# Sinkhorn reciprocals written to PSUM, sums made by accumulating DMAs, and a new order around the stream mixes of a two-layer attention and FFN kernel

## What is computed

```
x = x + fake_quant(LN(x)) @ fake_quant(ctx)                  # layer 1
x = x + mixed(LN(x)) + branch(LN(x))                         # layer 2
x = x + softmax((LN(x) Wq' + bq)(ctx Wk' + bk)' / 32) @ ctx  # layer 3
x = x + down(silu(gate(LN(x))) * up(LN(x)))                  # layer 4, hidden size 2752, low-rank terms added

# layer 2, per token, x_streams = LN(x) as 4 streams of 256:
H_res = sinkhorn_log(logits, 50 iterations, tau 0.1)         # 4x4, rows and columns normalised in turn
H_res = (1 - g) * I + g * H_res
x_mixed = einsum('btij,btjc->btic', H_res, x_streams)
y = einsum('btnc,btn->btc', x_streams, H_pre) @ W_branch
result  = x_mixed + einsum('btc,btn->btnc', y, H_post)
```

## Time and profile before

| | |
|---|---|
| time before | 1239.46 us, median of 3 runs (1236.49 to 1240.28) |
| the profiled execution's own time | 1237.51 us |
| its span, first to last instruction | 1235.7 us |
| TensorE busy (matmuls) | 1169.7 us, 95% |
| VectorE busy | 797.1 us, 65% |
| ScalarE busy | 479.5 us, 39% |
| GpSimd busy | 128.9 us, 10% |
| mean granted TensorE clock | 0.986 of full |

### The profile page before, as it was taken

How to read it: one execution, slowest core, us unless ns; L and a number is a source line. 1 busy time by engine, 2 the same in 40 slices (tenths; PEclk the granted TensorE clock), 3 DMA queues, 4 the chain that set the end, 5 groups by cost and what they waited for, 6 DMA issues and landing times.

```text
span 1235.7 us, 16385 instructions
## 1 busy us (share of the span) xinstructions
PE 1169.7 (95%) x6357; PEld 579.0 (47%) x6362; DVE 797.1 (65%) x1571; ACT 479.5 (39%) x716; POOL 128.9 (10%) x176
## 2 busy tenths in 40 slices
PE   3899999689999999999999999999999999999998
PEld 2345554454444445454444444444444444444444
DVE  6695898989997156887776776767767652222220
ACT  7782851574135124534434434334343231111110
POOL 4410260028002210020000000000001000000000
PEclk9989999899999999999999999999999999999999
DMA  9530000015012114220121121111111231111310
GB/s 370 208 115 1 1 1 1 0 69 152 19 36 100 49 35 139 69 101 24 46 69 68 36 69 44 59 69 34 69 52 24 71 136 46 46 47 46 119 38 26
DMA packets 26062, 83.58 MB, mean 68 GB/s; under 512 B 3648, under 2 KB 4288, under 8 KB 25984
## 3 DMA queue, kind: packets, MB, share of 16 engines
q1 hardware_dynamic: 25984, 82.53, 19.6%
HBM read 76.22 MB, written 6.29 MB: 67 GB/s over the span
## 4 chain that ended last, share of the span: by engine, by line
PE 75%; DVE 17%; ACT 5%; issue 2%; DMA 1%; ACTq 0%; SPq 0%; DVEq 0%
PE PAIR L2257 31%; PE PAIR L1894 11%; PE PAIR L1895 11%; PE PAIR L1896 11%; DVE LORA L1292 3%; DVE LORA L1291 3%; DVE LORA L1290 3%; DVE X L1338 2%; PE PAIR L1959 2%; PE PAIR L2214 2%; PE PAIR L1976 1%; PE PAIR L2091 1%; PE PAIR L1967 1%; PE PAIR L2269 1%; ACT POOL L617 1%
## 5 line engine op out<-in xcount | busy, mean ns | idle before, releaser
L1894 PE MATMUL PAIR<-POOL 128*128 128x512 f16 x688 | 261.3, 380 | 4.8 <-DVE POOL L1381 2.8
L1896 PE MATMUL PAIR<-POOL 128*128 128x512 f16 x688 | 261.3, 380 | 0.0
L1895 PE MATMUL PAIR<-POOL 128*128 128x512 f16 x688 | 261.3, 380 | 0.0
L2257 PE MATMUL PAIR<-XT,POOL 128*128 128x512 f16 (+1 forms) x1056 | 239.0, 379 | 1.0 <-ACT ST L867 1.0
L2257 PEld LDWEIGHTS PAIR<-XT,POOL 128*128 128x128 f16 (+1 forms) x1056 | 102.6, 98 | 120.5 <-issue 2.5
L2257 PE MATMUL PAIR<-X,POOL 128*128 128x512 f16 (+1 forms) x528 | 121.2, 379 | 0.0
L1896 PEld LDWEIGHTS PAIR<-POOL 128*128 128x128 f16 x688 | 67.2, 98 | 81.8 <-issue 0.6
L1894 PEld LDWEIGHTS PAIR<-POOL 128*128 128x128 f16 x688 | 67.1, 98 | 76.6 <-issue 5.5
L1895 PEld LDWEIGHTS PAIR<-POOL 128*128 128x128 f16 x688 | 67.2, 98 | 64.5 <-issue 0.8
L1509 DVE SCALAR_TENSOR_TENSOR STG<-STG,PAIR 128x1024 f32<-128x1024 f32 (+2 forms) x32 | 28.1, 884 | 92.1 <-PE PAIR L2269 89.1
L901 ACT ACTIVATE POOL<-STG 128x1024 f16<-128x1024 f32 (+2 forms) x32 | 25.0, 788 | 144.9 <-DVE STG L1509 144.9
(11 more groups left out here) (281 smaller groups left out, 1717.0 us busy)
## 6 DMA issues: line engine op xcount, KB each, us to landing
STG<-in_gate_w SPq DMA_DIRECT2D x21, 512.0 KB, 3.5
STG<-in_up_w SPq DMA_DIRECT2D x21, 512.0 KB, 4.2
STG<-in_ctx_t SPq DMA_DIRECT2D x16, 512.0 KB, 3.8
STG<-in_ctx SPq DMA_DIRECT2D x16, 512.0 KB, 3.6
STG<-in_down_w SPq DMA_DIRECT2D x16, 512.0 KB, 3.5
POOL<-in_ctx SPq DMA_DIRECT2D x12, 512.0 KB, 11.1
X<-in_x SPq DMA_DIRECT2D x8, 512.0 KB, 9.7
out_t<-X SPq DMA_DIRECT2D x16, 256.0 KB, 2.9
```

The costliest lines, as they stand in the source:

```text
L1894: e.matmul(dst, l_hi, r_hi, start=first, stop=False)
L1895: e.matmul(dst, l_hi, r_lo, start=False, stop=False)
L1896: return e.matmul(dst, l_lo, r_hi, start=False, stop=last)
L2257: i = e.matmul(dst, blk[:, a_, k, :], src[:, b_, k, :], start=(opens and k == 0 and n == 0), stop=(k == KD // 2 - 1 and n == 2), skip_grou ...
```

## The change

It has six parts.

1. The reciprocals of a Sinkhorn step go to `RP`, a part of `PAIR[2]` in PSUM, and the third instruction reads them there. `PAIR[2]` is therefore not used by `M` any more: its blocks take `PAIR[1]` and `PAIR[0]` in turn. The bank tables of the transposes and of `ctk` and `at` are changed to match, and `weights_transpose(2)`, the first user of `PAIR[2]` afterwards, waits for `hr_ok` 2.
2. `add_share` is one DMA issued by GpSimd that adds 512 KB from SBUF to `X` in SBUF; each waits for the one before (semaphore `summed`).
3. For tiles 4 and 5 ScalarE makes the products of `sj` 2 and 3 (`mix_help(4)`, `mix_help(5)`), and `add_helps` adds them to `X` by four more such DMAs. VectorE does only half of these two tiles' mixes.
4. Batch 0: VectorE does all four `mix` and then each tile's `mix_end` and statistics; ScalarE does `m_lo_of(6)`, `mix_help(0)`, `mix_diag(2)`, `m_hi_of(7)`, `mix_help(1)`, `bias_raw`, `mix_diag(3)`; on TensorE `m_rest(7)` stands ahead of `mix_product(3)`.
5. Batch 1: statistics and roots come in two pairs of tiles (4 and 5, then 6 and 7), later than before on VectorE; the numbers of second steps between the projections are 20, 11, 11, 11, 13, 2 where they were 27, 11, 11, 11, 6, 2.
6. GpSimd's `context_lo` is one instruction of 1024 columns where it was four of 256.

```diff
         def add_share(g):
             e.wait_ge(py_ok, g + 1)
-            for q in range(0, D, CST):
-                last = e.tensor_tensor(X[:, g, q:q + CST], X[:, g, q:q + CST], SHARE[g][:, q:q + CST], ALU.add)
-            last.then_inc(share_ok, 1)
+            if g:
+                e.wait_ge(summed, 16 * g)
+            e.dma_start(X[:, g, :], SHARE[g], accum_op=ALU.add).then_inc(summed, 16)
+
+        def add_helps(g):
+            e.wait_ge(mixed, g + 2)
+            for n in range(2):
+                e.wait_ge(summed, 16 * (NT + 2 * (g - BT) + 2 * n))
+                for t in range(2):
+                    e.wait_ge(help_ok, 2 * (g - BT + t) + n + 5)
+                    e.dma_start(X[:, g + t, :], XT1M[2 * t + n], accum_op=ALU.add).then_inc(summed, 16)
...
-        M_PAIR = (2, 1, 0, 2, 1, 0, 2, 1)
-        T3_PAIR = (1, 3, 0, 2)
+        M_PAIR = (1, 0, 1, 0, 1, 0, 1, 0)
+        T3_PAIR = (3, 0, 1, 3)
...
+            RP = PAIR[2][:, 0:n32]
             for n in range(JOINT):
-                sinkhorn_step(n, ZP, RS, RR)
+                sinkhorn_step(n, ZP, RS, RP)
...
-            for n, more in enumerate((27, 11, 11, 11, 6, 2)):
+            for n, more in enumerate((20, 11, 11, 11, 13, 2)):
...
             mix_product(2)
-            mix_product(3)
             m_rest(KD - 1)
+            mix_product(3)
```

More of the change, by code:

```diff
@@ L104, in __init__ @@
     def __init__(self, pairs, uses):
-        self.pairs = pairs
         self.uses = uses
         self.place = {use[0]: i for i, use in enumerate(uses)}
+        self.at = [use[3] if len(use) > 3 else pairs[i % len(pairs)] for i, use in enumerate(uses)]
     def pair(self, *name):
-        return self.pairs[self.place[name] % len(self.pairs)]
+        return self.at[self.place[name]]
     def wait_empty(self, eng, *name):
-        before = self.place[name] - len(self.pairs)
-        if before >= 0:
-            eng.wait_ge(self.uses[before][1], self.uses[before][2])
+        i = self.place[name]
+        for n in range(i - 1, -1, -1):
+            if self.at[n] == self.at[i]:
+                eng.wait_ge(self.uses[n][1], self.uses[n][2])
+                break
 def build(nc, x, ctx, ctx_t, consts, small_w, w_branch, wq, wk, bqk, gate_w, gate_tail, up_w,
@@ L529, in context_lo @@
                 e.wait_ge(c_hi, i + 1)
[L530 to L533, removed]
+                e.tensor_tensor(lo, STAGE[n % SLOTS], hi, ALU.subtract).then_inc(c_lo, 1)
             def zero(n):
@@ L580, in _ @@
                 context_lo(i)
+            add_helps(4)
             for i in range(2 * KP, 2 * KP + 6):
@@ L1059, in _ @@
             weights_hi(3)
-            norm_root(4, 8)
-            for g in range(4, 8):
-                third_normal(g)
+            norm_root(4, 6)
+            third_normal(4)
+            third_normal(5)
             third_hi(4)
             third_hi(5)
+            norm_root(6, 8)
+            third_normal(6)
+            third_normal(7)
             context_hi(16)
@@ L1326, in weight_lo, with mix @@
                                        ALU.subtract).then_inc(w_lo, 1)
-            def mix(g, sj0=0, sj1=None):
-                last = 2 if g < 2 else 1 if g < BT else NST
-                sj1 = sj1 or last
-                if sj0 == 0:
-                    e.wait_ge(share_ok, g + 1)
-                for sj in range(sj0, sj1):
+            def mix(g):
+                e.wait_ge(summed, 16 * (g + 1))
+                for sj in range(1 if 2 <= g < BT else 2 if g < BT + 2 else NST):
                     for si in range(NST):
@@ L1659, in _ @@
             mix_factors(0)
-            mix(0)
-            mix(1)
-            mix_end(0)
-            stats_of(0)
-            mix_end(1)
-            stats_of(1)
-            norm_ask(0, 2)
-            mix(2)
-            norm_rest(0, 2)
-            mix(3)
-            mix_end(2)
-            stats_of(2)
-            mix_end(3)
-            stats_of(3)
+            for g in range(BT):
+                mix(g)
+            for g in range(BT):
+                mix_end(g)
+                stats_of(g)
+                if g == 1:
+                    norm_ask(0, 2)
+                    norm_rest(0, 2)
             norm_ask(2, 4)
@@ L1712, in _ @@
             context_lo(11)
+            weights_sum(2)
             weights_lo(2)
@@ L1715, in _ @@
                 context_lo(i)
+            mixed_stats(4)
+            mixed_stats(5)
+            norm_ask(4, 6)
             weights_sum(3)
+            weights_lo(3)
+            norm_rest(4, 6)
+            mix(7)
+            add_attended(0)
             stats_of(6)
-            mix(7)
             stats_of(7)
-            norm_ask(4, 8)
-            weights_lo(3)
-            norm_rest(4, 8)
-            add_attended(0)
+            norm_ask(6, 8)
+            norm_rest(6, 8)
             stats_of(0)
@@ L2166, in weights_transpose @@
             def weights_transpose(g):
+                if g == 2:
+                    e.wait_ge(hr_ok, 2)
                 e.wait_ge(e_ok, g + 1)
```

104 lines of the change are left out of this document (56 added, 48 removed).

## The result

| | before | changed | changed, second set of runs |
|---|---|---|---|
| median | 1238.28 us (4 runs) | 1225.24 us (4 runs, 1221.11 to 1227.28) | 1227.70 us (4 runs, 1225.70 to 1228.72) |
| ratio to before, 95% interval | | 0.989 (0.9857 to 0.9924) | 0.9914 (0.9899 to 0.9929) |
| profiled span | 1235.7 us | 1221.9 us | 1226.4 us |

The account below looks back on a forecast made before the run. TensorE, 95% busy, was taken as the limit, its stages waiting for the Sinkhorn chains. Gains of 10.3 and 5.7, together 16.0 us, took the profiled 1237.5 to 1221.5; plus 1.95 for the median, 1223.5 us, range 1215 to 1235.

Parts of the forecast that it names:

- The collisions: Sinkhorn third instructions lengthened beside GpSimd: all excess goes, -8.9 us in batch 0's chain, -12.4 us in batch 1's.
- The PSUM operand at no cost: Sinkhorn steps: reading or writing reciprocals in PSUM was taken to add nothing, by a 151 ns copy row.
- The first stage: From the end of `M` (226.1 us) to the first projection (267.3 us): gain 10.3 us, bounds 8 to 12.
- 3.1 for `m_lo_of(7)`: Before the first projection: ScalarE no longer waits 3.12 us for `m_rest(7)`, which stood behind `mix_product(3)`.
- The loss behind ScalarE's queue: Before `third_normal(0)`: 2.8 of the first chain's 8.9 us are lost, 6.1 arrive.
- my fourth rival: The new order costs more than it gives (late VectorE, clock dip): 8 us gained, 1231 us; chance 0.10.
- The second stage: From the first projection to 500 us: -6.3 - 1.0 + 1.6 = -5.7 us, bounds -2 and -10.
- The new wait at the transpose of tile 6: `third_transpose(6)` needs `third_lo(4)`, which stands late on VectorE: about 1.6 us of new TensorE wait.
- The reason given for `attend(0)`: It still waits about 2.8 us: `context_hi(10)` behind `exponential(3)`, tile 14 and 15 loads after `context_lo(10)` and `(11)`.
- The accumulating DMAs: Adds of shares and help: 6 us each from issue to landing, covered by slack; slow-DMA rival 1244.5 us, chance 0.12.
- L: Accumulating DMA's time from issue to landing; from 8.4 us TensorE waits 2 us per further us, gain nil near 14.
- The range: Whole kernel, 1215 to 1235 us; low end: remaining 4.4 us of waits gone and first stage at 12.

Follow-up runs that it names:

- number 1: Reciprocals of a Sinkhorn step written to SBUF again, all else as in the changed kernel: 1243.2 us, ratio 1.0034.
- number 4: Only the reciprocals in PSUM, with the banks this needs, against the kernel before: 1221.3 us, ratio 0.9863.
- number 8: Changed kernel without the help and with shares added by GpSimd's tensor_tensor instructions instead of DMAs: 1228.9 us, ratio 0.9914.
- number 9: Changed kernel with each share's accumulating DMA cut into two halves, the second issued when the first has landed: 1243.6 us, ratio 1.0033.
- number 7: Changed kernel without the help; VectorE does all 16 products of tiles 4 and 5: 1224.7 us, ratio 0.9896.
- number 10: Kernel before with only the reciprocals in PSUM, plus three shifts (second-step counts, bias_raw, context_lo and context_hi order): 1229.9 us, ratio 0.9927.

## Why the prediction came out as it did

The time was 1.7 us over the forecast and inside its own range, in the direction that was given. That it is so near is in part luck: the gain is 13.0 us where 16.0 were forecast, the median of before fell by 1.2, and the second set stands 4.2 us over the forecast. In the first profile the two stages gave 16.5 us (B 9.0, C 7.5), the later start of the chain took 2.8 back, and the span fell by 13.8. Step by step:

*The collisions* (-8.9 us in the first chain): A went from 98.8 to 90.1, -8.7. Right, and by its mechanism (numbers 1, 4 and 8). In batch 1 the third instructions take 15.5 us in sum where they took 28.0, -12.5 for the -12.4 forecast; `mix_factors(1)` still came at 323.3 and not at 317, of which 4.1 us are the later first projection. *The PSUM operand at no cost*: the third instruction has a median of 224 ns against 226, the reciprocal 261 against 253. The 65 ns a step that the Trainium skill's errata ("VectorE: DVE Perf Modes", the section on the TRN2 errata) would have made of it are not there.

*The first stage* (-10.3): -9.0 by B. Up to `third_normal(0)` it gained 6.6 us (6.1 forecast), behind it 2.4, where 3.1 for `m_lo_of(7)` and 1.1 for the clock were counted. The clock gave nothing: it is 0.84 against 0.83, and TensorE's busy time in the stage 25.3 against 24.9 us. The loss behind ScalarE's queue was seen, but as the price of the chain's new end, and not as that of the new order: `m_lo_of(6)` ahead of the help. With the old order B is 11.0 us shorter than before. I had read the 2.8 us "lost behind ScalarE's queue" and the 3.1 us won at `m_lo_of(7)` in one sum; measured together the new order loses 2.0. That the new order costs more than it gives was my fourth rival, with 0.10; in this stage it is what happened.

*The start of the chain*: nothing in the prediction said that it can stand 2.8 us later with the same code. That is 2.8 of the 4.1 us between the forecast of the first projection (257.0) and the profile (261.07); the other 1.3 are the stage's.

*The second stage* (-5.7): C is 7.5 us less in the first profile and 2.6 in the second. In the profile of before TensorE's granted clock from 500 to 520 us was 0.91, in that of the changed kernel 1.00. Up to TensorE's next wait ahead of that, which ends at 500.7 and 488.4 us, the two stretches are 233.4 and 227.3 us long: -6.1 for what the change can reach. The new wait at the transpose of tile 6 is 2.3 us (1.6 forecast), that of `attend(0)` 2.5 (2.8), `projected_lo`'s is gone. The reason given for `attend(0)`, that `context_hi(10)` stands behind `exponential(3)`, holds for the changed kernel alone: before it stood ahead, a shift that the six parts of the change do not list, and the waits were 2.8 us all the same.

*The accumulating DMAs*: 4.6 us, taken as 6; covered, as said. But their danger was not where I put it. By the prediction TensorE waits from L = 8.4 us on, and it decides from L of about 14. In number 9, at some 7.5 us a tile, it already waited 3.4 us and the time was 1243.6; and with the reciprocals in SBUF it is 1243 to 1249 at 4.6 us. Most of this goes through holds of VectorE, of which my row of a collision (0.86 us for one GpSimd instruction) gave no sign.

*The range*: its low end of 1215 does not follow from its terms, 4.4 us of waits and 1.7 to the bound of 12, which give 1217.4.

*Help, counts, `context_lo` in one*: the help is nothing (number 7); the counts and `context_lo` in one were not tried alone.

What the twelve runs say of the change as a whole: its first part carries all of the gain. By the ratios the other five, together, take back 3 to 6 us of it (0.9863 for the first part alone, 0.989 and 0.9914 for all). The profiles do not bear out so much. The whole change has 2.0 us more in B, by the order of batch 0, and in its first profile 1.9 less in C, so that B and C together are 390.8 us against 390.7 for the first part alone. The rest of the difference between these two profiles lies ahead of the first reduction (131.2 and 127.9 us), where both do the same work. With the old order the changed kernel is at 0.9858, level with the first part alone. Whether the other parts cost anything beyond that order is open.

## What to carry over

Where two engines meet, ask of each small instruction on the chain what operands it has and what runs beside it; here one move of 32 columns to PSUM was worth 17 us, and moving a four-column instruction back by two pairs of `projected_lo` 2 to 4 us. A change that is safe only because of another part of the same change (DMAs issued by GpSimd, beside chains of VectorE) should be tried alone, with that part undone, before it is kept. When a chain gets shorter, look again at what was put in front of its end on the other engines: the order that suits the new end may be the old one.

## What was not expected of the hardware

An instruction of VectorE that is held beside GpSimd can be held for far longer than one of GpSimd's instructions. Seen so far: `scalar_tensor_tensor` with two tensor inputs in SBUF, mostly 0.63 to 0.87 us (1.5 to 2.1 beside instructions of 1024 columns), so one instruction of GpSimd, where GpSimd's records are 0.67 or 0.68 us at a cadence of 0.63, or 0.72 at 0.68; the same one for 3.1, 3.9, 3.9, 8.8, 15.2 and 15.2 us, to the end of GpSimd's block, where it had just issued accumulating DMAs and its records are much longer than their cadence (0.95 to 1.17 at 0.63, 2.42 at 2.09); `tensor_scalar` of four columns in SBUF with a scalar a partition for 4.4, 7.8, 7.8 and 9.7 us, to the end of the block, behind such DMAs (number 9) or without any (numbers 4, 8 and 10); and a copy of 64 columns within SBUF, once, for 0.60 us where the other took 0.18 (`take_apart` before). Never held: `projected_lo`, reductions, reciprocals, and the third instruction with the reciprocal in PSUM, 168 of 168 in each of the kernels that has it.

The Trainium skill ("GPSIMD Engine Reference", section Specifications) says that GpSimd shares its SBUF interfaces with VectorE, and names as contending VectorE's instructions that have two SBUF inputs or run in a mode of two ports. The Trainium skill ("SBUF — State Buffer", section Who interferes with whom) calls the sharing an exclusive lock. The `scalar_tensor_tensor` held here, and free with one input in PSUM (number 1 against the changed kernel), agrees with that; for the `tensor_scalar` and the copy it would have to be the mode, which no trace shows. How long one is held, and why a whole block of GpSimd can pass without a turn for VectorE, neither the pages nor these runs settle. The lengths of GpSimd's records are rough in these profiles; records that overlap by 0.3 us or more go with it in every case of the first kind, but the `tensor_scalar` was also held by blocks whose records overlap by 0.05 to 0.07 us (2.13 at 2.09, 0.70 at 0.63).
